# The last gate-and-up tile and the last three down tiles of a decoder block worked in two token halves

## The reference

```
x = x + attention(layernorm(x))                 # 32 heads, 8 key/value heads, causal, head size 128
x = x + cross_attention(ctx, ctx, layernorm(x)) # one 128x128 softmax per batch
x = x + ffn(layernorm(x))

def ffn(x):                                     # x: 1024 tokens x 512
    gate = x2 @ Wg                              # 512 -> 1376, W = (q - (z + 1)) * s, s per group of 128 rows
    up   = x2 @ Wu
    inter = gate * sigmoid(gate) * up
    return (inter @ Wd).astype(float16)         # 1376 -> 512, rounded to float16
```

## Time and profile before

| what | us |
|---|---|
| median of 3 runs | 765.29 |
| the profiled execution, its time | 766.75 |
| its span, first to last instruction | 764.9 |
| TensorE busy | 741.3 (97%) |
| VectorE, ScalarE, GpSimd busy | 509.7, 383.0, 308.2 |

### The profile page before, as it was taken

The page is one execution under the profiler, slowest core; times in us unless marked ns, Lnnn a source line. Parts: engine busy times, 40 slices in busy tenths (PEclk is TensorE's granted clock), DMA queues, the critical chain, the costliest instruction groups (busy, mean ns, idle before and its releaser), DMA issues.

```text
span 764.9 us, 11214 instructions
## 1 busy us (share of the span) xinstructions
PE 741.3 (97%) x3732; PEld 618.2 (81%) x3732; DVE 509.7 (67%) x669; ACT 383.0 (50%) x961; POOL 308.2 (40%) x334
## 2 busy tenths in 40 slices
PE   7999999999999999999999999999999969999995
PEld 7888888888888888888888888888887647888873
DVE  6457736864675577457736864675458868888897
ACT  3365526443553555265526443553556646555652
POOL 4352314322331332152314322331335534689876
PEclk9999999999999999999999999999999999999998
DMA  9412033212322040213023101303710002212002
GB/s 297 117 52 84 1 106 110 78 38 68 123 64 90 16 165 12 96 53 115 0 86 110 58 31 35 125 12 119 239 42 2 0 1 56 83 45 74 28 11 110
DMA packets 44351, 56.44 MB, mean 74 GB/s; under 512 B 7432, under 2 KB 26056, under 8 KB 44328
## 3 DMA queue, kind: packets, MB, share of 16 engines
q1 hardware_dynamic: 44328, 56.15, 22.7%
HBM read 45.26 MB, written 10.88 MB: 73 GB/s over the span
## 4 chain that ended last, share of the span: by engine, by line
PE 86%; DVE 4%; POOL 4%; issue 3%; ACT 2%; DMA 1%; POOLq 0%; SPq 0%; ACTq 0%
PE psum L442 20%; PE psum L444 20%; PE psum L443 20%; PE psum L558 7%; PE psum L617 5%; PE psum L618 5%; PE psum L567 3%; PE psum L639 2%; PE psum L640 2%; DVE stats L1074 1%; POOL o_sum L1035 1%; PE psum L462 1%; PE psum L448 1%; ACT probs L811 1%; DMA xacc<-in_x 1%
## 5 line engine op out<-in xcount | busy, mean ns | idle before, releaser
L990 POOL TENSOR_TENSOR probs<-probs,rowinv 128x512 f32<-128x512 f32 x64 | 71.1, 1111 | 307.8 <-DVE rowinv L1219 307.8
L811 ACT ACTIVATE probs<-probs,negmax 128x128 f32<-128x128 f32 x256 | 99.8, 391 | 60.5 <-DVE negmax L1206 60.5
L442 PE MATMUL psum<-xt_hi,wq_hi 128*128 128x512 f32 x256 | 104.4, 408 | 0.0
L804 ACT CAST pt_hi<-psum 128x512 fp32r<-128x512 f32 x64 | 37.5, 586 | 128.3 <-PE psum L567 128.3
L442 PE MATMUL psum<-wo_hi,at_hi 128*128 128x512 f32 x256 | 100.2, 391 | 0.5 <-DVE at_lo L1237 0.5
L444 PE MATMUL psum<-xt_hi,wq_lo 128*128 128x512 f32 x256 | 100.2, 391 | 0.0
L443 PE MATMUL psum<-xt_lo,wq_hi 128*128 128x512 f32 x256 | 99.9, 390 | 0.0
L444 PE MATMUL psum<-wo_hi,at_lo 128*128 128x512 f32 x256 | 99.7, 389 | 0.0
L443 PE MATMUL psum<-wo_lo,at_hi 128*128 128x512 f32 x256 | 99.6, 389 | 0.0
L1237 DVE TENSOR_TENSOR at_lo<-psum,at_hi 128x512 fp32r<-128x512 f32 x64 | 44.1, 689 | 71.9 <-ACT at_hi L838 71.9
L723 ACT ACTIVATE qt<-psum 128x512 f32<-128x512 f32 x64 | 38.0, 594 | 75.8 <-PE psum L444 74.1
(11 more groups left out here) (133 smaller groups left out, 1636.1 us busy)
## 6 DMA issues: line engine op xcount, KB each, us to landing
wq_raw<-in_L_attn_w_q SPq DMA_DIRECT2D x8, 1024.0 KB, 5.5
wo_raw<-in_L_attn_w_o SPq DMA_DIRECT2D x8, 1024.0 KB, 7.7
unpacked_w<-u_q SPq DMA_DIRECT2D x8, 688.0 KB, 3.0
gw<-unpacked_w SPq DMA_DIRECT2D x20, 256.0 KB, 3.5
unpacked_w<-u_q SPq DMA_DIRECT2D x6, 512.0 KB, 2.6
u_q<-in_L_ffn_gate_qweight SPq DMA_DIRECT2D x8, 344.0 KB, 7.0
u_q<-in_L_ffn_up_qweight SPq DMA_DIRECT2D x8, 344.0 KB, 3.8
u_q<-in_L_ffn_down_qweight SPq DMA_DIRECT2D x10, 256.0 KB, 3.3
```

Source lines behind the costliest of these rows:

```text
L442: pe.matmul(dst, a_hi, b_hi, start=start, stop=False)
L811: e = act.activation(probs[:, t % 2, j, :], probs[:, t % 2, j, :], ACT.Exp, bias=negmax[:, t % 2, j:j + 1], accum_out=rowsum[:, t % 2, j:j ...
L990: pool.tensor_tensor(probs[:, t % 2], probs[:, t % 2], rowinv[:, t % 2, :].unsqueeze(2).to_broadcast([P, HG, P]), ALU.mult).then_inc(prob_ ...
```

## The change

Everything before window 10 stays. Window 10, down tile 9 and down tile 10 are replaced by 40 "items" of one bank and 2 matmuls each, item i in bank i mod 8 (`d_last`, `gu_last`). TensorE's order is now: tile 10 half 0 (items 0 to 7), down 8 half 0 (8 to 11), tile 10 half 1 (12 to 19), down 9 half 0 (20 to 23), down 8 half 1 (24 to 27), down 10 half 0 (28 to 31), down 9 half 1 (32 to 35), the turning of blocks 0 to 3, down 10 half 1 (36 to 39), the turning of blocks 4 to 7. An item waits for the copy of the item 8 before it (`last_free`). Blocks 0 to 3 are turned into banks 0 and 2.

ScalarE, VectorE and GpSimd do the same steps as before on 512 tokens at a time. The product and the remainder of tile 10 are on GpSimd for half 0 and on VectorE for half 1. Chunk 0 of down 10 is closed by ScalarE and GpSimd in both halves, chunks 1 to 3 by VectorE. `Y_POOL` is (2, 3, 6), and the stores go in the order 0, 1, 4, 2, 5, 7, 3, 6. The diff, cut to its core:

```diff
+        FULL = NT - 1
+        Y_POOL = (2, 3, 6)
+        STORES = (0, 1, 4, 2, 5, 7, 3, 6)
+        def gu_last(h, k):
+            return (0, 12)[h] + k
+        def d_last(c, h, j):
+            return {NT - 3: (8, 24), NT - 2: (20, 32), NT - 1: (28, 36)}[c][h] + j
...
         @block.sync
-            for b in range(NB):
+            for b in STORES:
...
         @block.tensor
+            def last_free(i):
+                done, count = last_copied(i - NB) if i >= NB else copied(FULL - 1, GU + i // 2)
+                pe.wait_ge(done, count)
...
+            def turn_last(h):
+                pe.wait_ge(last_closed, h + 1)
+                done, count = last_copied(d_last(NT - 1, h, HC - 1))
+                pe.wait_ge(done, count)
+                done, count = last_copied(d_last(NT - 2, 1, 2))
+                pe.wait_ge(done, count)
...
+            last_gate_up(0)
...
+            last_down(NT - 3, 0)
+            last_gate_up(1)
+            pe.wait_ge(intlo_ready, NT - 1)
+            last_down(NT - 2, 0)
+            last_down(NT - 3, 1)
+            pe.wait_ge(last_lo[0], 1)
+            last_down(NT - 1, 0)
+            last_down(NT - 2, 1)
+            turn_last(0)
+            pe.wait_ge(last_lo[1], 1)
+            last_down(NT - 1, 1)
+            turn_last(1)
...
         @block.scalar
+            last_first(0)
+            inner_first(n - 1)
+            last_down_part(NT - 3, 0)
+            last_silu_half(0)
+            last_first(1)
+            last_inner_first(0)
+            last_down_part(NT - 2, 0)
+            last_silu_half(1)
+            last_down_part(NT - 3, 1)
+            last_inner_first(1)
+            last_close_part(0)
+            last_down_part(NT - 2, 1)
+            last_close_part(1)
             for i, b in enumerate(Y_POOL):
...
         @block.gpsimd
+            last_down_sum(NT - 3, 0)
+            pool.wait_ge(last_silu, 1)
+            pool.tensor_tensor(f_u[0:w, r, half(0)], f_g[0:w, r, half(0)], f_u[0:w, r, half(0)],
+                               ALU.mult).then_inc(last_inner[0], 1)
+            pool.wait_ge(last_hi, 1)
+            pool.tensor_tensor(int_lo[0:w, n % RING_I, half(0)], f_u[0:w, r, half(0)],
+                               int_hi[0:w, n % RING_I, half(0)].bitcast(F32), ALU.subtract).then_inc(last_lo[0], 1)
+            last_down_sum(NT - 2, 0)
+            last_down_sum(NT - 3, 1)
+            last_close(0)
+            last_down_sum(NT - 2, 1)
+            y_sum(0)
+            last_close(1)
+            y_sum(1)
+            y_sum(2)
...
         @block.vector
+            last_add(0)
+            last_down_add(NT - 3, 0)
+            last_add(1)
+            last_down_add(NT - 2, 0)
+            dve.wait_ge(last_silu, 2)
+            dve.tensor_tensor(f_u[0:w, r, half(1)], f_g[0:w, r, half(1)], f_u[0:w, r, half(1)],
+                              ALU.mult).then_inc(last_inner[1], 1)
+            last_down_add(NT - 3, 1)
+            dve.wait_ge(last_hi, 2)
+            dve.tensor_tensor(int_lo[0:w, n % RING_I, half(1)], f_u[0:w, r, half(1)],
+                              int_hi[0:w, n % RING_I, half(1)].bitcast(F32), ALU.subtract).then_inc(last_lo[1], 1)
+            last_close(0)
+            last_down_add(NT - 2, 1)
+            y_add(0)
+            y_add(1)
+            last_close(1)
+            for b in (4, 5, 7):
+                y_add(b)
```

More of the change, by code:

```diff
@@ L669, in _ @@
                     gate_up(n, c, 1)
-            for n in range(LAG, NT):
+            for n in range(LAG, FULL):
                 gate_up(n, 0, 0)
@@ new lines, in last_gate_up @@
+            def last_gate_up(h):
+                for k in range(GU):
+                    i = gu_last(h, k)
+                    last_free(i)
+                    c, m, w, r = k // 2, k % 2, width(FULL), FULL % RING_GU
+                    dst = psum[0:w, i % NB, :]
+                    pe.matmul(dst, gw[:, r, m, c, 0:w], ft_hi[:, c, half(h)], start=True, stop=False)
+                    pe.matmul(dst, gw[:, r, m, c, 0:w], ft_lo[:, c, half(h)], start=False,
+                              stop=True).then_inc(last_done, 1)
@@ L895, in down_part @@
                         d_s[:, j, c:c + 1]).then_inc(act_out, 1)
-            for n in range(NT + LAG - 1):
-                if 1 <= n < NT:
+            for n in range(FULL):
+                if n >= 1:
                     if n >= 2:
@@ L906, in _ @@
                     down_part(n - LAG, 0)
-                if n >= LAG:
                     down_part(n - LAG, 2)
[L909 to L917, removed]
+                w = width(n)
@@ new lines, in _, with last_first @@
+                done, count = copied(n, gu_at(n, GU - 2))
+                act.wait_ge(done, count)
+                act.activation(f_g[0:w, n % 2], f_g[0:w, n % 2], ACT.Silu).then_inc(silu_ready, 1)
+            n, w, r = FULL, width(FULL), FULL % 2
+            def last_first(h):
+                for m in range(2):
+                    i = gu_last(h, m)
+                    act.wait_ge(last_done, i + 1)
+                    act.mul((f_g, f_u)[m][0:w, r, half(h)], psum[0:w, i % NB, :], gu_s[0:w, m, n, 0:1]).then_inc(last_act, 1)
@@ new lines, in last_close @@
+            def last_close(h):
+                done, count = last_copied(d_last(NT - 1, h, 0))
+                pool.wait_ge(done, count)
+                pool.wait_ge(last_summed, last_sum_count(NT - 2, h, 0))
+                pool.tensor_tensor(o16[:, 0, half(h)], last_part[:, h], o_sum[:, 0, half(h)], ALU.add).then_inc(last_closed, 1)
+            n, w, r = FULL, width(FULL), FULL % 2
+            last_down_sum(NT - 3, 0)
+            done, count = last_copied(gu_last(0, GU - 1))
+            pool.wait_ge(done, count)
@@ L1299, in down_add @@
                                              ALU.mult, ALU.add).then_inc(dve_out, 1)
-            for n in range(1, NT):
+            for n in range(1, FULL):
                 for c in range(1, HC):
@@ new lines, in last_down_add @@
+            def last_down_add(c, h):
+                for j in (1, 3):
+                    i = d_last(c, h, j)
+                    dve.wait_ge(last_done, i + 1)
+                    done, count = copied(c + LAG - 1, d_at(c - 1, j)) if c == NT - 3 else last_copied(d_last(c - 1, h, j))
+                    dve.wait_ge(done, count)
+                    dve.scalar_tensor_tensor(o_sum[:, j, half(h)], psum[:, i % NB, :], d_s[:, j, c:c + 1],
+                                             o_sum[:, j, half(h)], ALU.mult, ALU.add).then_inc(last_dve, 1)
@@ new lines, in last_close @@
+            def last_close(h):
+                for j in range(1, HC):
+                    i = d_last(NT - 1, h, j)
+                    dve.wait_ge(last_done, i + 1)
+                    if j % 2:
+                        done, count = last_copied(d_last(NT - 2, h, j))
+                        dve.wait_ge(done, count)
+                    else:
+                        dve.wait_ge(last_summed, last_sum_count(NT - 2, h, j))
+                    dve.scalar_tensor_tensor(o16[:, j, half(h)], psum[:, i % NB, :], d_s[:, j, NT - 1:NT],
+                                             o_sum[:, j, half(h)], ALU.mult, ALU.add).then_inc(last_dve, 1)
```

162 lines of the change are left out of this document (92 added, 70 removed).

## The result

The changed kernel takes 768.20 us (median of 7 runs, 767.21 to 769.04) against 765.29 (7 runs, 764.0 to 766.9): ratio 1.0036, 95% interval 1.0024 to 1.0049. It is slower by 2.9 us, outside the range of 763.6 to 767.2. On another occasion it took 767.13 (12 runs) against 766.0 (29 runs): 1.0027, interval 1.0014 to 1.0039.

What follows compares the result with a forecast made beforehand. The end was bound by when stores flow without a gap, held back by TensorE's second turning. Stores from 758.9 to 760.1, one fewer left (-0.69), gave -0.15 to +1.05, middle +0.45: 765.7 us, range 763.6 to 767.2.

Steps and rivals of the forecast that it cites:

- the wait of VectorE's two operations with two SBUF inputs: VectorE's half 1 product and remainder each wait for one GpSimd step, costing GpSimd 1.1 us for the pair.
- the first turning: TensorE's transposes of blocks 0 to 3, forecast to start at 751.9 after standing over 3.5 us.
- GpSimd's list: GpSimd's steps from 738.6, back to back at 1.26 us, become the chain; half 0's closing ends at 751.8.
- The third store: Block 4's store, third in SyncE's list, forecast to be issued between 758.9 and 760.1.
- Rival B: Slower: VectorE's products also lose to GpSimd's next step, 1.27 us each, 2.5 on VectorE; 767.0 to 767.5; chance 0.17.
- VectorE's win at 748.95: Argument against rival B: in the kernel before, VectorE got its turn there though GpSimd had its next step ready.
- The ring: Eight items in flight, 3.73 us deep: TensorE's waits for free banks cost nothing, upper bound 0.5 us.
- The end: Last stores: six left in one flow, 6 x 0.69 + 1.75 = 5.9 us from block 4's issue to span end.
- The ranking of the lists: Among the engines' lists, GpSimd's becomes the chain; its half 0 closing ends 751.8, VectorE's 751.3.
- Rival C: Only blocks 0 and 1 leave while half 1 is multiplied; without any early store +1.8 us, 767.1; chance 0.04.
- The half clock: TensorE at 1.2 GHz over turning 0 and items 36 to 39: span end 766.0 against 764.8, middle 765.4 taken.
- The order of `y_sum(0)`: GpSimd adds block 2 to 756.2 before closing half 1 at 757.5, ahead of the second turning.

Runs made afterwards that it cites:

- the halved sums: Kernel before, with GpSimd's two sums of down 9 each cut into two steps of 512 tokens: 763.59 us, ratio 0.9978.
- yield sooner: All three edits, with GpSimd's first wait for VectorE moved one sum earlier: 764.15 us, ratio 0.9982.
- all three edits: Kernel after with GpSimd's two waits for VectorE, half 1 closed before block 2's addition, stores in order 0, 1, 2, 4, 3, 5, 7, 6: 762.96 us.
- the yields alone: Kernel after, with two waits added on GpSimd, for VectorE's product and remainder of half 1: 764.21 us, ratio 0.9983.
- 54 trials: Kernel before, with 19, 18 and 17 trials behind its last additions (three kernels), one VectorE operation during back-to-back GpSimd steps; kernel times mean nothing.
- the other store order: Kernel after, with stores in the order 0, 1, 2, 4, 3, 5, 7, 6: 767.13 us, ratio 1.0022.

## Why the prediction was wrong

**The step that failed** is the wait of VectorE's two operations with two SBUF inputs. I had them wait for one step of GpSimd each. The remainder waited for nothing, as GpSimd was idle by then; the product waited for the step in which it asked and three more, 5.08 us instead of 1.4. From it hang TensorE's pause at item 33, the wait of ScalarE's cast and of the closing copy behind it, GpSimd's 1.86 us, and the first turning, 2.1 us later than forecast (752.87; 751.9 less the 1.15 by which this execution was ahead is 750.8). It was VectorE's closing that released it, where I had GpSimd's list as the chain. The third store was issued 1.1 us later than the middle of its forecast (759.48 + 1.15 = 760.6; forecast 758.9 to 760.1), and the end moved with it. Rival B named this very mechanism, one more step for 1.27 us, with a chance of 0.17; it came as three for the product and none for the remainder. B's sum was also short: it put 2.5 us on VectorE's list, yet had half 0 closed only 1.8 later (753.1 for 751.3). What I held against B, VectorE's win at 748.95, was true of that place: the halved sums repeat it. My error was to carry an arbitration seen at one step end over to a run of five steps without a gap, and to take only one more loss as the other bound of its price; the wait's upper bound was the whole run that GpSimd had queued, 4.97 us.

**What held.** The ring: no wait up to item 32, and none at item 33 either once the product took 1.40 us ("yield sooner"). GpSimd's list: its remainder of half 0 was due at 743.1 - 1.15 = 741.95 and started at 741.94. The end: third store issued at 759.48, span end 5.92 later, forecast 5.9. The ranking of the lists: once VectorE gets in, GpSimd's sets the turnings. Rival C's reading of the stores: blocks 0 and 1 left ahead of the rest, the other six flowed at the end.

**The half clock** was a term of +0.6 in the middle of the forecast, half of the 1.2 us that I priced for turning 0 and items 36 to 39. In the profile it came sooner than that, over items 33 to 35 (749.61 to 753.03), as the pause did, and keeping it away changed neither tail nor median; so the term measured nothing here. Where it fell in other profiles differed. On the first turning it cost 0.7 us. On the second the transposes took 0.8 longer (1.89 for 1.07), but only the first four stand ahead of block 4's store, which was issued 1.37 us after the turning began instead of 1.16: 0.2.

**The order of `y_sum(0)`.** I had priced that order in the working (block 2 added, then half 1 closed) but named it no rival. With VectorE's wait settled it is the largest part of what is left: all three edits make the tail 1.9 us shorter than the yields alone. Of that, 1.2 is the second turning, 24.6 us after tile 10 (752.89 - 728.26) against 25.8 (756.13 - 730.33); 0.2 is the half clock on the other kernel's second turning; the other 0.5 is the order of the stores.

**What stays open:** why a gap ahead of GpSimd's run lets VectorE in at the next step end here and is not needed in 54 trials; and how large the loss is. The medians say 2.9 and 1.1 us, the tails 1.6. The tails hang on the one profile of the kernel before, in which the half clock lay on the path. Three kernels with trials run its code up to its last additions, and in them the second turning, 25.7 us after tile 10 in the profile before, starts after 25.0 to 26.8:

```profile
755.70 1.07 PE L723 MATMUL psum<-ident,o 128*128 128x128 f16 x16 [0.17 <-DVE o L1373]
754.97 1.05 PE L722 MATMUL psum<-ident,o 128*128 128x128 f16 x16 [0.27 <-POOL o L1081]
```

The first row (tile 10 at 730.72) is at full clock, the second (tile 10 at 728.21) has the half clock over all of down 10. So the tail of before may be 0.7 shorter or 1.0 longer than 33.5, while the kernel after's was 35.0 and 35.1. The half clock costs the kernel before up to 1.8 us, and over items 33 to 35 costs the kernel after nothing, which no sum of mine had. The yields take 4.0 from the median (768.20 to 764.21, on two occasions) and 2.0 from the tail; occasions differ by 1 us for the same kernel, and executions by up to 6.

## What to carry to other kernels

Cutting work into halves to shorten a pipeline's end also turns one long step of a neighbour into a row of short ones; a VectorE operation with two SBUF inputs beside such a row on GpSimd must be priced by the whole row, or GpSimd be made to wait for it at the point where its result is wanted (two waits, 2.0 us of the tail). The row did not keep VectorE out in every place, so this is a bound of the price and not a rule for it. Compare executions from a mark in the code near the change, not by their spans: here the spans said +0.5, the tails +1.6. And take more than one profile of either kernel: behind the same mark the kernel before still differed by 1.8 us with the clock.

## What the runs showed of the hardware

- A VectorE operation with two SBUF inputs and GpSimd's steps exclude each other, and a loser waits for whole steps: up to 5.65 us for a product that took 0.69 in a trial where GpSimd's step ended just as it asked. The Trainium skill, SBUF — State Buffer, section "SBUF: two separate sides", has the exclusion, and says that the one that starts first keeps the pair for its instruction; the traces agree for a single instruction, as the four sums beside the waiting product took 4.97 us, 1.24 each. Who is next when both stand ready differed: VectorE in all 54 trials, GpSimd three times in a row in the changed kernel, where the product took 5.08 us instead of 1.4.
- The same code ahead of the change differed by 3.3 us from execution to execution (728.21 to 731.47 for tile 10's first matmul).
- The granted clock of the same code differed too: 1.2 GHz over none, 3.4 us or all of down 10 in the kernel before's code, with the second turning 25.0, 25.7 and 26.8 us after tile 10.
- Stores of 256 KB at the end flow at 375 to 391 GB/s, 0.69 us each; once they queue, the span ends 1.75 us plus 0.69 for each store that is left, counted from the issue of the first of these; the sum taken from the kernel before (6.58 us for seven) held for the kernel after (5.92 for six, 5.9 by the sum) and for the other store order (5.17 for five, 5.2 by the sum).
